# A GRU with a routed expert layer: the opening loads regrouped on two queues, and the first input projections done weight by weight

## The reference, cut to what matters

```python
def cell(h, x):
    gi = x @ W_ih + b_ih
    gh = h @ W_hh + b_hh
    i_r, i_z, i_n = jnp.split(gi, 3, axis=-1)
    h_r, h_z, h_n = jnp.split(gh, 3, axis=-1)
    r = sigmoid(i_r + h_r)
    z = sigmoid(i_z + h_z)
    n = tanh(i_n + r * h_n)
    return (1.0 - z) * n + z * h
# hs = all 256 states, one after the other, for 16 sequences
# router: softmax of hs/|hs| @ router_w, the best two of eight, weights made to sum to 1
# out = x + sum over e of combine[:, e] * (hs @ Wa[e] @ Wb[e])
```

## Time and profile before

| what | value |
|---|---|
| time before, median of 3 runs | 1015.73 us (1015.42 to 1016.42) |
| the profiled execution, its own time | 1015.49 us |
| its span in the trace | 1013.7 us |
| outside the span | 1.8 us |
| start of the first `tr` of step 0 | 26.60 us |
| PE busy, share of the span | 97% |

### The profile page before, as it was taken

How to read it: one execution, slowest core, us unless ns; L and a number is a source line. 1 busy time by engine, 2 the same in 40 slices (tenths; PEclk the granted TensorE clock), 3 DMA queues, 4 the chain that set the end, 5 groups by cost and what they waited for, 6 DMA issues and landing times.

```text
span 1013.7 us, 60662 instructions
## 1 busy us (share of the span) xinstructions
PE 980.9 (97%) x28939; PEld 675.3 (67%) x20799; DVE 877.0 (87%) x3637; ACT 693.4 (68%) x2696; POOL 292.9 (29%) x755
## 2 busy tenths in 40 slices
PE   4689999999999999999999999999999999999997
PEld 2456677767667767666666666776676676676674
DVE  6889888888888888888888888888888888888887
ACT  6687766776666776676677676677666667766664
POOL 1032323332323332323332332332232332233223
PEclk9999999999999999999999999999999999999999
DMA  8321111111111111111111111101111111110000
GB/s 299 90 81 31 28 32 31 28 28 34 26 32 32 26 29 35 26 32 33 29 25 35 29 31 30 33 22 35 30 29 30 32 24 34 30 30 20 14 9 29
DMA packets 49361, 38.84 MB, mean 38 GB/s; under 512 B 34532, under 2 KB 38972, under 8 KB 49084
## 3 DMA queue, kind: packets, MB, share of 16 engines
q1 hardware_dynamic: 48236, 31.41, 11.4%
q10 hardware_dynamic: 848, 3.54, 1.0%
HBM read 18.94 MB, written 8.39 MB: 27 GB/s over the span
## 4 chain that ended last, share of the span: by engine, by line
PE 90%; DVE 5%; DMA 2%; ACT 1%; issue 1%; SPq 0%; POOL 0%; DVEq 0%; POOLq 0%
PE pairs L882 16%; PE ybank L882 11%; PE gates L962 11%; PE gates L967 11%; PE pairs L873 8%; PE ybank L873 5%; PE zbank L882 5%; PE zbank L873 5%; PE obank L882 5%; PE nbank L882 5%; PE obank L873 3%; PE nbank L873 2%; DMA whh<-in_L_cond_W_hh 1%; DVE tr L747 1%; DVE acc L830 1%
## 5 line engine op out<-in xcount | busy, mean ns | idle before, releaser
L882 PE MATMUL pairs<-wx,xs 128*32 128x384 f16 x4096 | 281.3, 327 | 0.0
L609 ACT ACTIVATE rr<-pre 128x64 f32<-128x64 f32 x256 | 65.7, 257 | 240.9 <-DVE pre L750 240.9
L882 PE MATMUL ybank<-hparts,wa 128*128 128x128 f16 x2048 | 194.0, 219 | 0.0
L882 PEld LDWEIGHTS ybank<-hparts,wa 128*128 128x128 f16 x2048 | 159.9, 98 | 29.8 <-issue 16.7
L873 PE MATMUL ybank<-hparts,wa 128*128 128x128 f16 x1024 | 178.3, 219 | 0.0
L463 POOL TENSOR_TENSOR y<-y 128x128 f16<-128x128 f32 x256 | 106.3, 435 | 249.3 <-ACT y L660 243.7
L873 PE MATMUL pairs<-wx,xs 128*32 128x384 f16 x2048 | 175.8, 326 | 0.0
L962 PE MATMUL gates<-whh,st 128*32 128x256 f16 x4080 | 158.6, 273 | 15.1 <-DVE st L778 14.7
L882 PEld LDWEIGHTS pairs<-wx,xs 128*32 128x32 f16 x4096 | 111.5, 96 | 91.4 <-issue 52.9
L962 PEld LDWEIGHTS gates<-whh,st 128*32 128x32 f16 x4080 | 104.4, 96 | 86.5 <-ACT gates L581 62.4
L967 PE MATMUL gates<-whh,hparts 128*32 128x256 f16 x4080 | 158.7, 273 | 0.0
(11 more groups left out here) (137 smaller groups left out, 1807.1 us busy)
## 6 DMA issues: line engine op xcount, KB each, us to landing
out<-outb SPq DMA_DIRECT2D x63, 128.0 KB
xin<-in_x SPq DMA_DIRECT2D x58, 128.0 KB
wih<-in_L_cond_W_ih ACTq DMA_DIRECT2D x4, 768.0 KB, 7.8
whh<-in_L_cond_W_hh SPq DMA_DIRECT2D x4, 768.0 KB, 11.7
wih<-in_L_ffn_Wb SPq DMA_DIRECT2D x8, 256.0 KB, 2.7
xs<-xh SPq DMA_TRANSPOSE x116, 3.0
wih<-in_L_ffn_Wa SPq DMA_DIRECT2D x4, 256.0 KB, 4.5
whh<-in_L_ffn_Wa SPq DMA_DIRECT2D x4, 256.0 KB, 2.7
```

The costliest lines, as they stand in the source:

```text
L609: nc.scalar.activation(rr[:, :], pre[:, RG, :, :].rearrange("p k b -> p (k b)"), ACT.Sigmoid, scale=1 / PROD_SCALE).then_inc(r_ready, 1)
L882: return nc.tensor.matmul(out, lhsT, rhs, start=start, stop=stop, skip_group_check=True)
```

## The change

SP now issues the four quarters of W_ih, the four of W_hh, the router and blocks 1 and 2 of x, with no wait among them. ACT issues the three biases (behind the wait for POOL's constants), then block 0 of x, and only then the table load and its first split; the four loads of the first state are issued by ACT behind its third weight piece. On PE, `put_first_biases` stands ahead of `turn_first(0)`, `first_parts` does each quarter for pairs 0 and 1, and blocks 1 and 2 are turned in steps 0 and 1. ACT runs `keep_biases` and `split_first(0)` behind piece 5 in place of piece 8 (block 0) and 12 (biases); DVE splits block 0 behind piece 5 as well. Blocks 1 and 2 are split by ACT in steps 0 and 1 (before: ahead of step 0, and in step 0), and by DVE in steps 1 and 2 (before: 0 and 1).

```diff
 # SP
-            sp.wait_ge(consts_ready, 2)
-            sp.dma_start(bias_h[0:P:32, HN, :], b_hh[2 * D:3 * D].rearrange("(j c) -> j c", j=K)).then_inc(bias_loaded, 16)
-            sp.dma_start(bias_h[0:P:32, RG:ZG + 1, :], b_hh[0:2 * D].rearrange(groups, g=2, j=K)).then_inc(bias_loaded, 16)
-            sp.dma_start(bias_i[0:P:32, :, :], b_ih.rearrange(groups, g=3, j=K)).then_inc(bias_loaded, 16)
-            for j in range(K):
-                sp.dma_start(cond_sb[32 * j:32 * j + B, :], cond[:, j * P:(j + 1) * P]).then_inc(cond_loaded, 16)
+            for k in range(K):
+                load_ih(k)
             for k in range(K):
                 load_hh(k)
             sp.dma_start(rw32[:, :, :], router_w.rearrange("(p k) e -> p k e", k=K)).then_inc(rw_loaded, 16)
             for b in (1, 2):
-                sp.wait_ge(whh_loaded[b], 16)
                 load_first(b)
 # ACT, first instructions
-            for k in range(K):
-                if k == 2:
-                    act.dma_start(xin[:, 0, :], x_blocks[0]).then_inc(first_loaded[0], 16)
-                act.dma_start(wih32[:, k, :, :].rearrange("p g n -> p (g n)"), W_ih[k * P:(k + 1) * P, :]
-                              ).then_inc(wih_loaded[k], 16)
+            load_biases()      # waits for consts_ready 2, then the three loads that SP had
+            act.dma_start(xin[:, 0, :], x_blocks[0]).then_inc(first_loaded[0], 16)
 # ACT, among the 24 pieces
             for n in range(N_GRU_SPLITS):
                 split_weights(n)
-                if n == 8:
+                if n == 2:
+                    load_cond()
+                if n == 5:
+                    keep_biases()
                     split_first(0)
                 if n == N_IH_SPLITS:
-                    keep_biases()
                     copy_high(-1)
...
-            split_first(1)
 # ACT, beside(n)
-                if n == 0:
-                    split_first(2)
+                if n + 1 < FIRST:
+                    split_first(n + 1)
 # DVE, beside(n), and among the 24 pieces
-                if n < FIRST - 1:
-                    split_first(n + 1)
+                if 1 <= n < FIRST:
+                    split_first(n)
...
-                if n == 8:
+                if n == 5:
                     split_first(0)
 # PE
                 pe.wait_ge(weights_split, splits_before(3 * (k + 1)))
-                pair_part(0, range(3 * k, 3 * k + 3))
+                for p in range(2):
+                    pair_part(p, range(3 * k, 3 * k + 3))
...
-                if p < T // 2:
-                    pair_part(p, range(UNITS[s]) if n % 2 else range(UNITS[s - 1] if n else 6, UNITS[s] if n else all_units))
+                if n and p < T // 2:
+                    pair_part(p, range(UNITS[s]) if n % 2 else range(UNITS[s - 1], UNITS[s]))
...
+                if n == 1:
+                    turn_first(2)      # at the end of wide_step
...
                 if n == 0:
-                    turn_first(2)
+                    turn_first(1)      # at the end of grouped_step
...
+            put_first_biases()
             pe.wait_ge(ident_step, 2)
             turn_first(0)
-            put_first_biases()
             wait_turned(0)
             for k in range(K):
                 first_parts(k)
-            pair_part(1, range(6))
-            turn_first(1)
             first_state_part()
```

More of the change, by code:

```diff
@@ L376, in beside, with load_ih @@
                     store(i - 2, s - 5)
-            sp.wait_ge(consts_ready, 2)
-            groups = "(g j c) -> j g c"
-            sp.dma_start(bias_h[0:P:32, HN, :], b_hh[2 * D:3 * D].rearrange("(j c) -> j c", j=K)).then_inc(bias_loaded, 16)
-            sp.dma_start(bias_h[0:P:32, RG:ZG + 1, :], b_hh[0:2 * D].rearrange(groups, g=2, j=K)).then_inc(bias_loaded, 16)
-            sp.dma_start(bias_i[0:P:32, :, :], b_ih.rearrange(groups, g=3, j=K)).then_inc(bias_loaded, 16)
-            for j in range(K):
-                sp.dma_start(cond_sb[32 * j:32 * j + B, :], cond[:, j * P:(j + 1) * P]).then_inc(cond_loaded, 16)
+            def load_ih(k):
+                sp.dma_start(wih32[:, k, :, :].rearrange("p g n -> p (g n)"), W_ih[k * P:(k + 1) * P, :]
+                             ).then_inc(wih_loaded[k], 16)
+            for k in range(K):
+                load_ih(k)
             for k in range(K):
@@ L549, in _, with load_biases, load_cond @@
         def _(act):
-            for k in range(K):
-                if k == 2:
-                    act.dma_start(xin[:, 0, :], x_blocks[0]).then_inc(first_loaded[0], 16)
-                act.dma_start(wih32[:, k, :, :].rearrange("p g n -> p (g n)"), W_ih[k * P:(k + 1) * P, :]
-                              ).then_inc(wih_loaded[k], 16)
+            groups = "(g j c) -> j g c"
+            def load_biases():
+                act.wait_ge(consts_ready, 2)
+                act.dma_start(bias_h[0:P:32, HN, :], b_hh[2 * D:3 * D].rearrange("(j c) -> j c", j=K)).then_inc(bias_loaded, 16)
+                act.dma_start(bias_h[0:P:32, RG:ZG + 1, :], b_hh[0:2 * D].rearrange(groups, g=2, j=K)).then_inc(bias_loaded, 16)
+                act.dma_start(bias_i[0:P:32, :, :], b_ih.rearrange(groups, g=3, j=K)).then_inc(bias_loaded, 16)
+            def load_cond():
+                for j in range(K):
+                    act.dma_start(cond_sb[32 * j:32 * j + B, :], cond[:, j * P:(j + 1) * P]).then_inc(cond_loaded, 16)
             def split_weights(n):
```

## The result

The changed kernel takes 1021.38 us (median of 6 runs, 1020.55 to 1021.90), the one before 1015.41 us on the same chip (6 runs, 1014.92 to 1016.42). The ratio is 1.0057, 95% interval 1.0044 to 1.0070: slower, by the 0.2% that the prediction took as its limit. Forecast were 1019.1 us, a range to 1021.2, and "slower" with a chance of 0.65; the median lies 0.2 us above the range's upper end. The profiled execution took 1020.55 us, the fastest of the six. It is 5.06 us above the profiled execution of the kernel before, while the medians lie 5.97 us apart: 0.9 us of that distance is in neither trace. The mean granted clock of the five other runs is 0.992 to 0.994, against 0.995 in the profiled one.

A forecast was written before the change was run, and what follows sets the result against it. Step 0's start, 26.60 us before, was taken to count, now set by the biases' landing: 10.0 + 19.6 - 26.6 = +3.0, plus 0.6 in step 2, on 1015.49 makes 1019.1 us; 8-in-10 range 1015.6 to 1021.2.

The forecast's parts named there:

- The mechanism: Opening: ACT and DVE stand behind piece 5 until PE has put the biases and turned block 0, eighteen pieces still left.
- biases landed, t: Opening: biases land at t = 10.0 us, bounds 5.9 and 12.6; break-even for the start at 7.0.
- bias products: PE, opening: products of the biases take 5.74 us, as read from the rows before.
- turn, high part, to DVE's low part: Opening: PE turns block 0 (0.75 with hand-over), ACT makes its high part; DVE's low part starts at t + 7.1.
- DVE, 19 slots, first state: DVE, opening: block 0's low part and eighteen weight pieces at 0.604 each, plus first state; ends at t + 19.2.
- last products, hand-over: PE, end of opening: last eight state products and hand-over take 0.4 us, putting `tr` at t + 19.6.
- the rival that had the biases at 5.9: Opening: biases land soon, t from 5.9 to 8.5, time 1015.0 to 1017.6 us, no measurable change; chance 0.27.
- Block 0 late: Rival, opening: block 0 lands at 17.6, after the bias products, time 1021.0 us; chance 0.10, within "slower".
- What is removed: Opening: the wait for block 1 of x goes, worth 0.6 us; SP's waits for W_hh go too.
- Step 2: DVE: one more block split ahead of `tr` costs +0.6 us, bounds 0.4 and 0.7.
- The rival that cut 5.74 to 3.4 by the ratio of the clocks: Opening: bias products at their fastest save 2.3 us, time 1013.4 with t = 5.9; part of "faster", chance 0.08.
- The weights: Opening: same bytes on full DMA engines, so the last W_hh quarter still lands at about 21.0 us.

The follow-up runs named there:

- e8_all_early: Changed kernel, but SP issues block 0, two W_ih quarters, first state, then the rest; ACT only biases; work reordered to suit; 1014.67 against 1015.15 us before.
- the filled version: Changed kernel plus unread PE products: 52 in the first state products, 24 in step 0, 36 in step 3; 1019.81 us, ratio 1.0042 to before.
- e4_no_sp_wait: Kernel before the change, with only SP's two waits for W_hh ahead of blocks 1 and 2 removed; 1015.88 us, ratio 1.0002.
- e3_late_places: Changed kernel with ACT's keep_biases and split_first(0) and DVE's split_first(0) behind piece 11 instead of 5; 1024.79 us, ratio 1.0086 to before.

## Why the prediction was right, and where it was off

**The total.** Forecast were +3.0 for the start and +0.6 for the steps, +3.6 in all. The profiled executions lie 5.06 us apart (+3.90 at the start, +0.45 in step 2, +0.80 in step 4), the medians 5.97. The direction and the mechanism were right; the size was too small by 1.5 to 2.4 us. Two terms that stood at nothing make up most of that: the wait for block 0 (0.96) and the lower clock behind the lengthened step (0.80). That the sum was not further off is in part luck, as the biases came 0.61 earlier than assumed.

**The mechanism** was the one forecast: ACT idle behind its sixth piece (from 10.1 to 15.49, forecast 11.5 to 16), DVE with eighteen pieces left when block 0 arrives. The sum for the start, term by term:

| term | forecast, us | profile after, us |
|---|---|---|
| biases landed, t | 10.0 | 9.39 |
| bias products | 5.74 | 6.06 (to 15.45) |
| wait for block 0 | 0 | 0.96 |
| turn, high part, to DVE's low part | 1.36 | 1.29 (16.41 to 17.70) |
| DVE, 19 slots, first state | 12.15 | 12.30 (to 30.00) |
| last products, hand-over | 0.4 | 0.50 |
| start of `tr` | 29.6 | 30.50 |

**The landing of the biases** was misread, though its error was small and on the other side. I took 10.7 from a wait of 0.2 us that the view gave to `bias_i`. PE was busy with block 0's turn up to there. In the kernel with the order alone, with the same queues, PE was free, and the products began at 9.34. A short wait behind other work bounds a landing from above only. That changing the queue leaves the landing alone was right: 9.34 from SP's queue, 9.39 from ScalarE's, 6.1 and 5.8 us after the issue of `bias_i`. The first state, too, took 6.5 to 7.2 us behind the biases on SP's queue, but 9.0 (median) behind block 0 on ScalarE's; in `e8_all_early` it took 6.0 on SP's, behind block 0 and two quarters of W_ih. What sets this is open. The rule of the Trainium skill ("DMA: Bandwidth & Descriptors", Queues, rings and completion order), read with single rows as packets as the prediction did, went with the rival that had the biases at 5.9; no run shows that.

**Block 0 late** was one of my rivals (0.10, landing at 17.6). It landed at 16.3, 12.2 us after its issue, where I had taken its old 8.2. It no longer stood behind two weight quarters in its own queue, but was issued when SP's queue held the four quarters of W_ih and was getting those of W_hh (issued from 2.99 to 5.12). Issued as the first transfer of all it was there at 5.8 (`e8_all_early`).

**What is removed.** "Taking away the wait alone is worth about 0.6 us" was wrong as far as it means SP's wait: its removal was worth nothing, since block 1 landed at 23.6 all the same. What may be worth something is the place of `turn_first(1)` on PE; no run tests it alone. In the changed kernel such a gain could not come to bear, because DVE ended at 30.00.

**Steps.** Step 2: forecast +0.6 with bounds 0.4 and 0.7; 0.45 measured. That the longer step 2 is followed by a longer idle stretch of PE, and that products behind it may run at 1.2 GHz, I had not seen: 0.80 us in step 4. This term is missing from my sum, and the filled version puts it, together with spells in other steps, at about 1.5 us. What decides whether the clock falls there stays open, since it did not in two kernels with the same stretch.

**A sign that did not hold.** "If PE's clock is already at the higher level during the bias products, the 5.74 is too large." It was at that level before and after, and they took 6.06 us all the same. The windows of 4 us after:

```profile
12.00:16.00 4.00, 3.45 (x6) 1.25 (x4) 0.00 (x0) 0.49 (x1) 0.00 (x0) 1.00 1.02 317
```

The rival that cut 5.74 to 3.4 by the ratio of the clocks therefore had no ground in the rows, though shorter products do occur (4.1 us in `e4_no_sp_wait`, also at 1.00). One slip in the rivals changes nothing: with t = 7 the sum gives 1016.1, not 1015.9.

**The weights.** Neither engine waited for a W_hh quarter in the changed kernel, so the assumption that they come at the old time did not bind.

## What to carry to other kernels

When two engines work through a list in a fixed order, ask of every operation in the list not when it could run first, but when what it needs will have landed; ahead of that time it holds everything behind it. Here, moving such an operation by itself uncovered two other waits (`e3_late_places`), while moving it together with the transfers brought the start to 24.65 (`e8_all_early`). So look at the transfers too: what is waited for first should be issued first, since the same 256 KB block took from 5.1 to 15.5 us to land, depending on what had been issued before it. And count the idle stretches that an edit leaves on TensorE, as the work behind them may run at half the clock.

## What the runs showed that was not expected

- The clock falls in the opening and the first steps, at places that differ from kernel to kernel even where the same idle stretches stand ahead. A step whose PE work fits at 2.4 GHz took 4.45 to 4.78 us at 1.2 GHz in place of 3.65 to 3.72. Added products that nobody needs made the kernel with the lowest median and the narrowest spread, though its lead over the same kernel without them is small (0.55 us).
- A 256 KB block took 5.1 us from issue to use as the first transfer (0.72 to 5.78), 8.2 us behind two quarters of W_ih in its queue, 12.2 us when issued at 4.11 behind three small ones on the less loaded queue, and 15.5 us when issued at 8.12 behind four quarters of W_hh in its queue and the W_ih in the other.
- The float32 bias products took 6.06 us in the changed kernel and about 4.1 us (10.84 to 15.00) in the run without SP's waits, with the same instructions: there two products of the last kind took 0.90 and 0.81 us, in the changed kernel 1.49 and 1.21. The granted clock does not tell them apart: it reads 1.00 in every window from 9 to 15 us in both. The cause stays open.
